# A graph layer in float32: half of the node pairs turned by VectorE instead of TensorE, and correction rows added in PSUM

## The reference

```python
msg = x[src]
agg = segment_sum(msg, dst, num_segments=n)
deg = segment_sum(ones, dst, num_segments=n)
mean = agg / maximum(deg, 1.0)[:, None]
h = mean @ W_l + b + x @ W_r
y = x + h * sigmoid(h)
out = (y - mean(y)) / sqrt(var(y) + 1e-5)
```

## Time and profile before

| | |
|---|---|
| median of three runs | 1616.02 us (1615.95 to 1616.12) |
| profiled execution | 1616.76 us, its span 1615.0 us |
| TensorE matmul busy | 1574.8 us, 98% |
| VectorE busy | 1408.7 us, 87% |
| ScalarE busy | 1028.8 us, 64% |
| GpSimd busy | 947.9 us, 59% |
| HBM traffic | 288.78 MB read, 139.67 MB written |
| granted TensorE clock, mean | 0.994 |

### The profile page before, as it was taken

How to read it: one execution, slowest core, us unless ns; L and a number is a source line. 1 busy time by engine, 2 the same in 40 slices (tenths; PEclk the granted TensorE clock), 3 DMA queues, 4 the chain that set the end, 5 groups by cost and what they waited for, 6 DMA issues and landing times.

```text
span 1615.0 us, 24709 instructions
## 1 busy us (share of the span) xinstructions
PE 1574.8 (98%) x7886; PEld 1311.1 (81%) x7886; DVE 1408.7 (87%) x2174; ACT 1028.8 (64%) x1433; POOL 947.9 (59%) x1089
## 2 busy tenths in 40 slices
PE   7998899999999999999999999999999999999996
PEld 5887688888888888888888888888888888888884
DVE  7988799999996888888888888888888888888886
ACT  4443343333335777777777777777777777777775
POOL 6446566666654665655566556665556656666563
PEclk9999999999999999999999999999999999999998
DMA  5456589888884676766667666666667666677674
GB/s 186 147 163 189 170 262 266 263 265 262 266 250 150 220 230 201 237 211 216 223 208 227 218 213 219 219 221 213 222 212 228 217 210 231 205 228 221 205 235 152
DMA packets 204245, 350.52 MB, mean 217 GB/s; under 512 B 37020, under 2 KB 51126, under 8 KB 204117
## 3 DMA queue, kind: packets, MB, share of 16 engines
q1 hardware_dynamic: 156135, 274.22, 51.6%
q0 software_dynamic: 46944, 74.22, 16.7%
q10 hardware_dynamic: 1038, 0.50, 0.1%
HBM read 288.78 MB, written 139.67 MB: 265 GB/s over the span
## 4 chain that ended last, share of the span: by engine, by line
PE 95%; DVE 2%; DMA 1%; issue 1%; SPq 0%; ACT 0%; POOL 0%; POOLq 0%; DVEq 0%
PE pH L473 81%; PE pT L567 9%; PE pT L541 3%; PE pT L482 1%; DMA light_h<-in_x 0%; DVE w_sum L799 0%; DVE w_sum L794 0%; DVE sums L923 0%; DMA light_x<-in_x 0%; PE pH L500 0%; PE pH L503 0%; DVE stats L1001 0%; SPq L246 0%; DVE row_mask L790 0%; DVE Z L794 0%
## 5 line engine op out<-in xcount | busy, mean ns | idle before, releaser
L473 PE MATMUL pH<-ws_hi,x_hi 128*128 128x512 f32 x1564 | 629.1, 402 | 0.0
L473 PE MATMUL pH<-ws_hi,x_lo 128*128 128x512 f32 x1564 | 611.4, 391 | 0.0
L473 PE MATMUL pH<-ws_lo,x_hi 128*128 128x512 f32 x1564 | 609.4, 390 | 0.0
L383 POOL DMA_INDIRECT cor<-correction_rows,node_idx x347 | 366.2, 1055 | 313.3 <-ACT cor L671 229.8
L708 ACT ACTIVATE x_hi<-pT 128x1024 fp32r<-128x1024 f32 x174 | 178.1, 1024 | 272.7 <-PE pT L567 272.7
L473 PEld LDWEIGHTS pH<-ws_hi,x_lo 128*128 128x128 f32 x1564 | 293.6, 188 | 63.3
L473 PEld LDWEIGHTS pH<-ws_lo,x_hi 128*128 128x128 f32 x1564 | 294.7, 188 | 54.5
L473 PEld LDWEIGHTS pH<-ws_hi,x_hi 128*128 128x128 f32 x1564 | 294.2, 188 | 54.5 <-issue 0.3
L986 DVE TENSOR_TENSOR Z<-pH,cor 128x1024 f32<-128x1024 f32 x174 | 212.5, 1221 | 100.4 <-PE pH L473 94.6
L717 ACT ACTIVATE O<-Z,shift,rstd 128x512 f32<-128x512 f32 x347 | 261.9, 804 | 3.2 <-DVE shift L1011 3.2
L1001 DVE BATCH_NORM_STATS2 stats<-Z 128x6 f32<-128x512 f32 x347 | 221.4, 680 | 0.0
(11 more groups left out here) (132 smaller groups left out, 1785.6 us busy)
## 6 DMA issues: line engine op xcount, KB each, us to landing
X<-in_x SPq DMA_DIRECT2D x173, 512.0 KB, 4.2
out<-O SPq DMA_DIRECT2D x173, 512.0 KB, 5.1
correction_rows<-c_out SPq DMA_DIRECT2D x98, 256.0 KB, 4.2
light_x<-in_x SPq DMA_DIRECT2D x66, 256.0 KB, 5.0
light_h<-early_product SPq DMA_DIRECT2D x44, 256.0 KB, 5.7
out<-light_o SPq DMA_DIRECT2D x44, 256.0 KB, 5.5
join_row<-joined SPq DMA_DIRECT2D x98, 64.0 KB, 4.1
light_h<-in_x SPq DMA_DIRECT2D x22, 256.0 KB, 2.9
```

What stands on the lines that cost most here:

```text
L383: g.indirect_dma_start(out=out_, out_offset=None, in_=table, in_offset=bass.IndirectOffsetOnAxis(ap=idx, axis=0), bounds_check=bound, oob_ ...
L473: last = mm(ps, a[:, k], w[:, k], start=(n == 0), stop=(n == len(terms) - 1))
```

## The change

- For every pair with t odd except the last one, TensorE no longer transposes. SyncE loads the pair a second time with four DMAs (`load_blocks`), each taking 128 columns of 256 rows into 32 partitions, 512 bytes at a time, into `x_raw`. VectorE turns all 32x32 blocks with one instruction (`turn_blocks`) into `x_blocks`. ScalarE and VectorE round and split from there. The features then stand in another order on the partitions and in K; a second copy of the summed weights with its rows in that order (`wb_hi`, `wb_lo`) is loaded, summed (GpSimd), rounded (ScalarE) and split (GpSimd) in the early stage, in memory that `wl_raw` and `rowed_f` had. Odd pairs multiply by it.
- From pair 2 on ScalarE copies the correction rows into `pH` before the matmuls (`seed`), the matmuls add onto them, and silu reads `pH`. `add_cor` remains for pairs 0 and 1. `cor` is reset and gathered three pairs ahead instead of two. On ScalarE the order in a step is now silu, rounding, seed, reset, light, normalise.
- `x_hi` and `x_lo` have K ahead of the tile of the pair.
- Early tiles from 28 on (`LATE`) are loaded six ahead into eight buffers in `X`. The load of tile 1 is issued behind the first of four pairs of weight loads. TensorE's small steps for the edge list stand one tile later. The first turns, masks and the carry stand one tile earlier; `find_nodes` and its matmuls are moved from edge tile 2 and from ahead of edge tile 0 to edge tiles 6 and 4; one VectorE column step more stands ahead of the first scan.
- The last steps of the node stage are in another order.

```diff
+        xs = sb("xs", [P, 4, D], f32)
+        x_raw, x_blocks = xs[:, 0:2], xs[:, 2:4]
...
+        wb_raw = wl_raw
+        wb_lo, wb_hi = sb("wb_lo", [P, K, D], f32r), sb("wb_hi", [P, K, D], f32r)
...
+        def by_blocks(t):
+            return t % 2 == 1 and t < NP - 1
+        def turned_by_pe(t):
+            return t // 2 + 1 + t // (NP - 1)
+        def in_blocks(tile):
+            return tile[:].rearrange("p k a (i r) -> p (a i) k r", r=32)
...   SyncE
+                if t + 2 < LATE:
+                    single(t + 2, load_early)
+                if t + 6 == LATE:
+                    sp.wait_ge(rows_moved, 2)
+                if LATE <= t + 6 < EARLY:
+                    single(t + 6, load_early)
...
-            single(1, load_early)
+                if k == 0:
+                    single(1, load_early)
...
             peeled(0, 8, move_early)
+            sp.wait_ge(wl_split, K)
+            for w, tile in ((w_l, wb_raw), (w_r, xs)):
+                for i in range(4):
+                    sp.dma_start(tile[32 * i:32 * i + 32], w[i * P:(i + 1) * P].rearrange("(k a) n -> a k n", a=32)
+                                 ).then_inc(wb_in, 16)
...
+            def load_blocks(t):
+                wait(sp, blocks_turned, (t + 1) // 2 - 1)
+                first = BASE + 2 * t * P
+                for j in range(4):
+                    sp.dma_start(x_raw[32 * j:32 * j + 32].rearrange("r a (i c) -> r (a i) c", i=4),
+                                 x[first:first + 2 * P, j * P:(j + 1) * P].rearrange("(i r) c -> r i c", r=32)
+                                 ).then_inc(blocks_in, 16)
...
                     load_light(0)
+                    sp.wait_ge(diff_made, ET)
+                    load_blocks(1)
...
             def move(t, q, u):
+                if by_blocks(t + 3):
+                    load_blocks(t + 3)
                 shifted(t, q, u, 3, NP, load_x)
...   GpSimd
+            pool.wait_ge(wb_in, 128)
+            for k in range(K):
+                g.tensor_tensor(wb_raw[:, k], wb_raw[:, k], xs[:, k], ALU.add).then_inc(wb_summed, 1)
+                single(14 + k, split_early)
+            peeled(18, 20, split_early)
+            for k in range(K):
+                pool.wait_ge(wb_rounded, k + 1)
+                g.tensor_tensor(wb_lo[:, k], wb_raw[:, k], wb_hi[:, k].bitcast(f32), ALU.subtract).then_inc(wb_split, 1)
+                single(20 + k, split_early)
...
+            single(2, gather_cor)
             def serve(t, q, u):
-                shifted(t, q, u, 2, NP, gather_cor)
+                if u == 0:
+                    light_at(q - 1, light_make_rstd)
                 shifted(t, q, u, -2, NP, make_rstd)
-                light(q, u)
+                shifted(t, q, u, 3, NP, gather_cor)
+                if u == 2:
+                    light_at(q + 1, gather_light)
...   TensorE
-            peeled(4 * FIND_ROUND + 5, 4 * FIND_ROUND + 8, early_tile)
+            peeled(4 * FIND_ROUND + 6, EARLY - 2, early_tile)
...
-            peeled(4 * FIND_ROUND + 8, EARLY - 1, early_tile)
+            single(EARLY - 1, transpose_early)
             single(0, turn)
-            single(EARLY - 1, early_tile)
+            single(EARLY - 2, early_matmuls)
             single(1, turn)
+            single(EARLY - 1, early_matmuls)
...
             def transpose_x(t, q, u):
+                if by_blocks(t):
+                    return
...
+                if t == 4:
+                    mark_rows_before()
...
-                wait(pe, z_made, t - 1)
+                else:
+                    pe.wait_ge(seeded, t - 1)
+                w_hi, w_lo = (wb_hi, wb_lo) if by_blocks(t) else (ws_hi, ws_lo)
                 for a in range(nt):
+                    last = three(pH[b][0:rows, a, :], x_hi[b][:, :, a, 0:rows], x_lo[b][:, :, a, 0:rows],
+                                 w_hi, w_lo, onto=t >= 2)
...   ScalarE
+            def seed(t, q, u):
+                nt, rows = pair_shape(t)
+                b, used = ring(q, u, 4)
+                wait(act, silu_made, t - 1)
+                if nt == 2:
+                    act.wait_ge(cor_in[b], 32 * (used + 1))
+                else:
+                    act.wait_ge(cor_in[b], 32 * used + 16)
+                a_(pH[u % 2][0:rows, 0:nt], cor[b][0:rows, 0:nt], ACT.Copy).then_inc(seeded, 1)
...
             def node_pair(t, q, u):
-                shifted(t, q, u, 2, NP, reset_cor)
+                shifted(t, q, u, -1, NP, silu)
                 shifted(t, q, u, 1, NP, round_x)
-                shifted(t, q, u, -1, NP, silu)
+                if t >= 1:
+                    shifted(t, q, u, 1, NP, seed)
+                shifted(t, q, u, 3, NP, reset_cor)
                 light(q, u)
                 shifted(t, q, u, -3, NP, normalise)
...   VectorE
-            loop_cols(0, col_bits - 3)
+            loop_cols(0, col_bits - 2)
             single(0, scan)
-            loop_cols(col_bits - 3, col_bits)
+            single(2, subtract)
+            loop_cols(col_bits - 2, col_bits - 1)
+            single(0, split_sums)
+            loop_cols(col_bits - 1, col_bits)
...
+            def turn_blocks(t, q, u):
+                dve.wait_ge(blocks_in, 64 * ((t + 1) // 2))
+                if t > 1:
+                    dve.wait_ge(lo_made, t - 1)
+                v.transpose(x_blocks, x_raw).then_inc(blocks_turned, 1)
...
             def node_pair(t, q, u):
-                shifted(t, q, u, -1, NP, add_cor)
+                if t == 1 or t == 2:
+                    single(t - 1, add_cor)
                 shifted(t, q, u, -2, NP, moments)
                 shifted(t, q, u, 1, NP, split_x)
                 shifted(t, q, u, -1, NP, residual)
                 shifted(t, q, u, -2, NP, make_shift)
                 light(q, u)
+                if by_blocks(t + 2):
+                    single(t + 2, turn_blocks)
```

More of the change, by code:

```diff
@@ L472, in three @@
                         pe.wait_ge(arriving, k + 1)
[L473 removed]
+                    last = mm(ps, a[:, k], w[:, k], start=(n == 0 and not onto), stop=(n == len(terms) - 1),
+                              skip_group_check=onto)
                 return last
             def transpose_early(t, q, u):
[L478 to L479 removed]
+                b = u % 2
+                tile, arrived, count = early_x(t)
+                pe.wait_ge(arrived, count)
                 wait(pe, early_copied, t - 1)
                 for k in range(K):
[L482 removed]
+                    last = nc.tensor.transpose(pT[b][:, 0, k * P:(k + 1) * P], tile[:, k * P:(k + 1) * P], eye)
                 last.then_inc(early_transposed, 1)
```

145 lines of the change are left out of this document (86 added, 59 removed).

## The result

The changed kernel takes 1561.2 us (1560.37 to 1561.54, 4 runs), the kernel before 1616.07 us: a ratio of 0.9655 [0.9641, 0.9669], 55 us faster. Forecast were 1542 us, with a range from 1530 to 1580. The direction and the range hold; the likeliest range, 1530 to 1555, doesn't. The gain is 19 us smaller than forecast; the experiments look for those 19 us.

What follows compares the result with a forecast made beforehand. TensorE was taken to bound the kernel. Terms of -75.7 (transposes), -3 (start and early to edge), +7 (edge to node) and -2 (tail) sum to -73.7, 1542 us against the median 1616.02; range 1530 to 1580.

Steps and rivals of the forecast that it cites:

- the likeliest range: Whole kernel: the forecast 1542 us with its small terms moving it from 1530 to 1555; chance 0.66.
- the seam: Early to edge stage: reordering saves 10.4 us, row marks and find_nodes cost some back, net 6.
- The steady stage: Node stage: eight transposes of 0.88 us go from 86 pairs, 75.7 us less; two pairs take 11.80 us.
- (a): Node stage: ScalarE becomes the bound if block rounding runs at half pace, +35, 1577 us; chance 0.12.
- (b): Node stage: waits for cor, X or blocks return as DMA is 90% busy, 1560 to 1600 us; chance 0.13.
- the matmuls stay 24 per pair: Node stage: matmuls adding onto rows already in PSUM keep count, shape and pace, priced at nothing.
- price and place: Node stage, VectorE: block transpose about 1.22 us, last in its step and hidden; load falls 0.6 us a pair.
- (c): Node stage: costly block packets make DMA the bound, slower than before from 64 ns a packet; 1672 at 74; chance 0.07.
- tile 1's gain: Start: tile 1's load goes ahead of six weight loads, worth 1 us, 0 to 2.
- 0 to 8: Early stage: a tile load behind the second weights' 2 MB lands 5 to 8 us late at worst, from 0; taken as +4.
- Edge to node: Into the node stage: the seed gates the third block and block loads delay it 2 us more, +7, between 0 and 10.
- The tail: End of kernel: the addition falls out of the last pairs' chain, -2 us, between 0 and -4.

Runs made afterwards that it cites:

- seed_only: Changed kernel with TensorE transposing every pair and only the first weights used, the seed kept: 1621.3 us.
- ws_for_odd: Changed kernel with odd pairs multiplying by the first weights instead of the second, so their output is wrong: 1552.2 us.
- wb_low: Changed kernel with the second weights' loads spread over eight early tiles and their tiles allocated right behind wl_lo: 1543.6 us, ratio 0.9544.
- one_block_load: Changed kernel with only pair 1's blocks loaded and the same data turned for all later odd pairs: 1563.4 us.
- the two shifts: Changed kernel with a 32-byte tile per partition allocated ahead of s_hi (1559.6 us) or ahead of everything (1562.05 us).
- blocks_only: Changed kernel without the seed, VectorE adding the correction rows as in the kernel before: 1670.3 us.
- spread loads: Changed kernel with the second weights' eight loads issued behind early tiles 8 to 15 instead of all in one: 1556.7 us, ratio 0.9639.
- blocks_late: The kernel with spread loads, first block loads issued after the last correction row's store, last two pairs finished in the old order: 1552.2 us.

## Why the prediction was right, and where it was off

Stage by stage, from landmarks of the two profiled executions (the row marks are in the edge stage now; the forecast had counted them into the seam):

| stretch | before, us | after, us | difference | forecast |
|---|---|---|---|---|
| to edge tile 0's first matmul | 179.69 | 177.28 | -2.4 | -3, with the next row |
| edge stage, to the transposes of pair 0 | 316.2 | 320.65 | +4.4 | in the -3 |
| from there to the block of pair 2 | 17.4 | 20.0 | +2.6 | +7, with the next row |
| block of pair 2, next transposes | 6.35 | 8.20 | +1.9 | in the +7 |
| from pair 3's block to the last matmul | 1078.8 | 1018.0 | -60.8 | -75.7 |
| last matmul to the end | 16.6 | 15.4 | -1.2 | -2 |

**The steady stage** is where it failed: -60.8 for -75.7. (The kernel as a whole lies in the stated range because that was drawn wide, for rivals (a) and (b); neither came about, and the likeliest range was missed.) The count was right (transposes in every second gap, 0.87 to 0.88 us each, gone); 84 of them lie in this stretch, 73.9 us. The step that failed is "the matmuls stay 24 per pair ... I price it at nothing". I had looked at whether adding onto PSUM changes the pace (it doesn't: the even blocks are seeded too and go at 0.227, and with every block seeded and the first weights alone, in `seed_only`, a block takes the 5.46 us of before) and not at the other thing that changes in the same line of code, the tile they stream. 85 odd blocks at 5.61 instead of 5.46 us in the chain cost 12.8, and 73.9 - 12.8 = 61.1 is the measured 60.8. `ws_for_odd` and `wb_low` show it by the tiles and by their place; `one_block_load` excludes the traffic, and the two shifts exclude the alignment for all but 0.001 us of it. What it is about the place stays open.

**ScalarE** (rival (a)): 22.5 us of four pairs' 23.6 were forecast, which is 0.95, and 0.95 it is, of 23.9; TensorE never waits for it. The block rounding is 3% dearer, not 100%. With the faster odd blocks it is at 0.96 and still keeps up.

**VectorE**: right, price and place. `blocks_only` shows how much hung on it: with the addition left on VectorE the kernel is slower than before. The prediction had no rival for the change's halves apart, and its account of VectorE is of busy time alone; there the waits inside its order were 1.1 us of 13.2.

**DMA** (rivals (b), (c)): the size was off, 45 ns a packet for 25 to 37. The rule of the Trainium skill's "SBUF — State Buffer", section on the DMA port swizzle, which I had priced at 50, came closer than the row I took; in the shape that writes all partitions the packet measured 30. Rival (b) named 45 to 60 ns as the price at which waits would come back. The price came true and the waits didn't: 0.95 of the DMA engines' time leaves TensorE without a wait. Landings hardly grew: x takes 4.5 us from issue to landing for 4.2 before, the gathered correction rows 5.2 for 4.2, and the prediction had x asked for 7.4 us ahead. The measured time lies within (b)'s 1560 to 1600 for another reason. Rival (c)'s threshold of 64 ns was not put to the test by a price between; at twice the packets (90 ns of DMA time for each packet of the change) the kernel takes 1675 us, where the prediction had 1672 for 74 ns. That these two are close is luck: by the prediction's own formula 90 ns makes 8.6 + 5.8 = 14.4 us in two pairs and a time near 1764. Two pairs took 13.3.

**The start.** Forecast +4 for the second weights (+3 with tile 1's gain), measured +7.8 at the merge: the load that is wanted stands behind eight more issues and behind 2 MB, and TensorE waits 8.16 us for it, at the upper end of "0 to 8". Behind this wait hides a second delay that the prediction didn't have: with the loads spread and the wait gone, the merge still ends 4.3 us later than before (2.1 to 5.2 in the four kernels with spread loads), and the chain ahead of it is VectorE's search. The seam itself came as worked out: from the merge to edge tile 0 it takes 24.0 us instead of 34.3, 10.2 saved for 10.4, and the row marks and `find_nodes` in the edge stage take 4.4 back, as forecast (10.4 to a net 6). So the whole miss, +2.0 us at the first node transposes against -3, lies ahead of the merge. The scatter of edge tile 0's start between executions (3 us, see the spread loads) bears on all of these.

**Edge to node.** The path was named rightly (store, gathers, landing, seed, block), only smaller: 4.6 us at pair 2's block for -3 + 7 = +4, by two errors that cancel (+2.0 for -3 ahead of the first node transposes, +2.6 for +7 behind them). The term "four block loads ahead of the last two stores delay all of it by 2 us more" was wrong: `blocks_late` shows no delay. Not forecast were the 1.9 us that the block of pair 2 takes longer at the lower clock, behind the idle stretch.

**The tail.** -2 forecast, -1.2 measured, made of -3.4 for the shorter chain and +2.2 for the new order.

## What to carry to other kernels

When a change gives an instruction another operand, the pace of that instruction is a term of the sum, even where its shape and count stay: compare start-to-start distances tile by tile, since busy shares don't show it. Where TensorE is the bound, try the operands at other places in the memory: the second weights lower down were worth 11 to 13 us here for no other edit, and with 32 bytes ahead of the edge stage's tiles that stage took 317.7 us in place of 320.65. Moving work between engines is a chain of trades: see that each engine that receives is unloaded first, and count the waits inside its order, not only its busy time.

## What the runs showed of the hardware

- The distance of 128x512 matmuls is 0.2345 us with the weights at bytes 212800 to 229184 of the partition and 0.227 us at 70304 to 86688. The edge stage's matmuls (`wl` low, `s_hi` and `s_lo` above byte 190000) go at 0.2332, and at 0.2296 once `s_hi` and `s_lo` stand 32 bytes further, at the same remainder modulo 64 as `wl`; with all tiles shifted alike they stay at 0.2332. Two places of the second weights were tried; the rule behind it is open.
- A packet of 512 bytes takes 30 ns of a DMA engine's time when a transfer writes 128 partitions and 45 ns when it writes 32.
- DMA busy for 0.95 to 0.97 of the window makes TensorE wait for less than 1 of 900 us here; at twice the block loads the share reads 1.11, which is over one, so the share is not to be read as a strict fraction near its limit.
- A ScalarE copy of 128x1024 from SBUF into PSUM takes 1.02 us, and matmuls that add onto rows written so go at the pace of before (`seed_only`: 5.46 us a block). A VectorE transpose of all 32x32 blocks of 128x1024 takes 1.23 us.
- Where TensorE had been idle for 3.1 to 4.5 us ahead of the first seeded or turned block (ten kernels), 5 to 11 of the block's first matmuls start about 0.43 us apart, the 1.2 GHz level.
